# The router's logits with x as the stationary operand, in a mixture-of-experts kernel

## The reference

```python
logits = xf @ gate_w.T
scores = jax.nn.softmax(logits, axis=-1)
topv, topi = jax.lax.top_k(scores, K)        # K = 2
gates = topv / jnp.sum(topv, axis=-1, keepdims=True)
...
valid = loc < cap
flat_idx = jnp.where(valid, topi * cap + loc, 0)
...
h = jax.nn.relu(jnp.einsum('ecd,ehd->ech', de, fc1_w) + fc1_b)
eo = jnp.einsum('ech,ehd->ecd', h, fc2_w) + fc2_b
out = jnp.sum(eo.reshape(E * cap, Dm)[flat_idx] * (gates * w)[:, :, None], axis=1)
```

## Time and profile before

| | us |
|---|---|
| three runs: 1414.11, 1414.88, 1414.97; median | 1414.88 |
| the profiled execution | 1415.69 |
| its span, first to last instruction | 1413.7 |
| PE busy in the span | 1378.0 |
| last matmul of the logits ends | 42.92 |

### The profile page before, as it was taken

One profiled execution on the slowest core, in us unless ns is written; L12 is line 12 of the kernel. 1 busy time (PEld: TensorE's weight loads), 2 busy tenths in 40 slices (PEclk: granted clock), 3 DMA queues, 4 the chain that ended last, 5 costly groups with the idle time before them and its releaser, 6 DMA issues.

```text
span 1413.7 us, 18054 instructions
## 1 busy us (share of the span) xinstructions
PE 1378.0 (97%) x6175; PEld 1131.0 (80%) x6175; DVE 1053.3 (75%) x1582; ACT 705.0 (50%) x1058; POOL 314.6 (22%) x333
## 2 busy tenths in 40 slices
PE   8679999999999999999999999999999999999997
PEld 6458888888888888888888888888888888888885
DVE  6898779687877778687886878687796868865443
ACT  5456455544555445455464455454455454644442
POOL 1174203320125103221034202241032200220021
PEclk9799999999999999999999999999999999999998
DMA  8677666656457555566466565575465533543232
GB/s 286 252 175 180 131 129 178 156 115 140 106 164 172 133 99 157 150 133 146 88 187 164 106 136 133 144 162 137 90 179 148 110 75 67 156 119 69 52 104 74
DMA packets 449676, 194.41 MB, mean 138 GB/s; under 512 B 398464, under 2 KB 401673, under 8 KB 447794
## 3 DMA queue, kind: packets, MB, share of 16 engines
q1 hardware_dynamic: 427378, 125.98, 40.5%
q0 software_dynamic: 22208, 67.29, 15.3%
HBM read 153.47 MB, written 39.98 MB: 137 GB/s over the span
## 4 chain that ended last, share of the span: by engine, by line
PE 95%; DVE 3%; DMA 1%; issue 1%; ACT 0%; SPq 0%; POOL 0%; POOLq 0%
PE ps L1253 15%; PE ps L1257 15%; PE ps L1263 15%; PE ps L1228 14%; PE ps L1229 14%; PE ps L1230 14%; PE ps L1171 1%; PE ps L1244 1%; PE ps L1245 1%; PE ps L1246 1%; DVE yfull L958 1%; PE ps L1151 1%; PE ps L1152 1%; DMA x_all<-in_x 0%; DVE yfull L971 0%
## 5 line engine op out<-in xcount | busy, mean ns | idle before, releaser
L1228 PE MATMUL ps<-yc_hi,w1c_hi 128*128 128x512 f32 x896 | 349.5, 390 | 1.2 <-DVE yc_lo L924 1.2
L1230 PE MATMUL ps<-yc_hi,w1c_lo 128*128 128x512 f32 x896 | 348.7, 389 | 0.0
L1229 PE MATMUL ps<-yc_lo,w1c_hi 128*128 128x512 f32 x896 | 348.6, 389 | 0.0
L1253 PE MATMUL ps<-w_hi,h_hi 128*128 128x512 f32 x952 | 254.4, 389 | 0.0
L1257 PE MATMUL ps<-w_hi,h_lo 128*128 128x512 f32 x952 | 254.4, 389 | 0.0
L1263 PE MATMUL ps<-w_lo,h_hi 128*128 128x512 f32 x952 | 254.4, 389 | 0.0
L1263 PEld LDWEIGHTS ps<-w_lo,h_hi 128*128 128x128 f32 x952 | 178.7, 188 | 37.2
L1253 PEld LDWEIGHTS ps<-w_hi,h_hi 128*128 128x128 f32 x952 | 178.7, 188 | 37.1
L1257 PEld LDWEIGHTS ps<-w_hi,h_lo 128*128 128x128 f32 x952 | 178.7, 188 | 37.0
L1228 PEld LDWEIGHTS ps<-yc_hi,w1c_hi 128*128 128x128 f32 x896 | 168.1, 188 | 39.2 <-DVE yc_lo L924 2.2
L1230 PEld LDWEIGHTS ps<-yc_hi,w1c_lo 128*128 128x128 f32 x896 | 168.2, 188 | 35.3
(11 more groups left out here) (182 smaller groups left out, 1506.4 us busy)
## 6 DMA issues: line engine op xcount, KB each, us to landing
w_raw<-in_L_ffn_fc_w SPq DMA_DIRECT2D x232, 256.0 KB, 3.0
w_raw<-in_L_ffn_fc_w SPq DMA_DIRECT2D x512, 64.0 KB
slots_dram<-x_blk POOLq DMA_DIRECT2D x28, 512.0 KB, 3.8
x_blk<-slots_dram SPq DMA_DIRECT2D x224, 64.0 KB, 2.6
out<-x_all SPq DMA_DIRECT2D x8, 1024.0 KB, 13.0
x_all<-in_x SPq DMA_DIRECT2D x6, 1024.0 KB, 13.7
b_bc<-in_L_ffn_fc_b POOLq DMA_DIRECT2D x8, 256.0 KB, 3.8
x_all<-in_x SPq DMA_DIRECT2D x4, 256.0 KB, 3.8
```

Of the source, the lines that this page charges most:

```text
L1228: pe.matmul(bank, hi, yc_hi[:, y, q, :], start=first and q == 0, stop=False, skip_group_check=True)
L1229: pe.matmul(bank, hi, yc_lo[:, y, q, :], start=False, stop=False, skip_group_check=True)
L1230: ins = pe.matmul(bank, lo, yc_hi[:, y, q, :], start=False, stop=last and q == 1, skip_group_check=True)
L1253: pe.matmul(eo_s[:, b, :], h_hi[:, c, blk], w2_hi[:, w, :], start=False, stop=False, skip_group_check=True)
```

## The change

In the x stage the operands change places: each 128 tokens of `xT_hi` and `xT_lo` become the stationary operand and the 16 columns of `grot_hl` the moving one. A unit then has eight matmuls with 16 columns for two with 512, and the logits come out with tokens on the partitions, each in its place of the bank. `keep_logits`, `turn_logits` and their semaphores go. The last chunk's logits go to another bank (`logits_last`), so that DVE can sum the first seven chunks before it.

Beside it: the tables of the comparisons are bf16 (`wt_bf`, `first_f`, `chosen`); the scan and the counts ahead are done for each choice by itself; the last of the four parts is cut in two; SP holds the loads of w1's third pair of tiles until the gathered rows are in; `w1_low_parts(1, 0)` goes ahead of `rotate_ps(0)`; in the first two groups some banks change (`bank_c11`, `bank_p5`), the seed of group 1 and its second product come earlier, one seed of fc2's output comes later, and the fifth product of group 1 waits for `h_ready` 3.

```diff
+    PARTS = ((0, 0, JH), (0, JH, TJ), (1, 0, JH), (1, JH, TJ - JH // 2), (1, TJ - JH // 2, TJ))
...
+        def bank_c11(G):
+            return BANK_P5 if G == 1 else BANK_C11
+        def bank_p5(G):
+            return BANK_P5 if G else BANK_FIRST
...
             load_w1(1)
+            for arrived in x0_in:
+                sp.wait_ge(arrived, 16)
             load_w1(2)
             cut_x(0)
...
-                if u % Q == Q - 1 and u >= Q:
-                    keep_logits(u // Q - 1)
-            keep_logits(CHUNKS - 1)
+            act.wait_ge(xT_used, UNITS)
...
             seed_c11(0)
+            seed_c11(1)
...
+                    if G == 1:
+                        act.wait_ge(c12_done, 1)
+                        seed_eo(0, SB - 1)
...
-            dve.wait_ge(logits_T, CHUNKS)
-            link(dve.tensor_reduce(lg[:, :, :], logits_hl.rearrange("p j a e -> p j e a"), X, ALU.add))
+            for g, js, parts in ((CHUNKS - 1, slice(0, TJ - XC), logits_hl[:, 0:TJ - XC]),
+                                 (CHUNKS, slice(TJ - XC, TJ), logits_last)):
+                dve.wait_ge(xT_used, g * Q)
+                link(dve.tensor_reduce(lg[:, js, :], parts.rearrange("p j a e -> p j e a"), X, ALU.add))
+                link(dve.reduce_max(mx[:, js], lg[:, js, :], X))
...
-                link(dve.tensor_tensor(wt[:, :, :], wt[:, :, :], first_bc, ALU.mult))
+                link(dve.tensor_tensor(wt_bf, wt_bf, first_bc, ALU.mult))
...
+                dve.tensor_tensor_scan(cnt[:, k * E:(k + 1) * E, :].rearrange("p e j -> p (e j)"),
...
+            for k in range(TOPK):
+                of_k = slice(k * E, (k + 1) * E)
+                dve.wait_ge(ahead_ready, k + 1)
+                link(dve.tensor_tensor(cnt[:, of_k, :], cnt[:, of_k, :], ahead_ps[k].unsqueeze(2).to_broadcast([P, E, TJ]), ALU.add))
+                ins = dve.tensor_tensor(loc[:, of_k, :], cnt[:, of_k, :], hot[:, k, :, :], ALU.mult)
...
+            w1_low_parts(1, 0)
             rotate_ps(0)
-            w1_low_parts(1, 0)
             rotate_ps(1)
...
+            y_low(0, T3, y12)
             y_sum(0, 3)
-            y_low(0, T3, y12)
...
-                pe.matmul(bank, grot_hl[:, q, :], xT_hi[:, u % XBUF, :], start=(q == 0), stop=False)
-                pe.matmul(bank, grot_hl[:, q, :], xT_lo[:, u % XBUF, :], start=False, stop=(q == Q - 1)).then_inc(xT_used, 1)
+                for t in range(XC):
+                    at = (u // Q * XC + t) * 2 * E
+                    to = xp_all[:, at:at + 2 * E] if u < UNITS - Q else hp[:, 0, t * 2 * E:(t + 1) * 2 * E]
+                    tokens = slice(t * P, (t + 1) * P)
+                    pe.matmul(to, xT_hi[:, u % XBUF, tokens], grot_hl[:, q, :], start=(u in (0, UNITS - Q) and t == 0), stop=False,
+                              skip_group_check=True)
+                    ins = pe.matmul(to, xT_lo[:, u % XBUF, tokens], grot_hl[:, q, :], start=False, stop=(q == Q - 1), skip_group_check=True)
+                ins.then_inc(xT_used, 1)
...
             pe.wait_ge(counts_ready, 1)
-            pe.matmul(ahead_ps, before[:, :], cnt[:, :, TJ - 1], start=True, stop=False)
-            pe.matmul(ahead_ps[:, E:2 * E], ones[:, :], cnt[:, 0:E, TJ - 1], start=False, stop=True).then_inc(ahead_ready, 1)
+            pe.matmul(ahead_ps[1], ones[:, :], cnt[:, 0:E, TJ - 1], start=True, stop=False)
+            pe.matmul(ahead_ps[0], before[:, :], cnt[:, 0:E, TJ - 1], start=True, stop=True).then_inc(ahead_ready, 1)
+            pe.wait_ge(counts_ready, 2)
+            pe.matmul(ahead_ps[1], before[:, :], cnt[:, E:2 * E, TJ - 1], start=False, stop=True).then_inc(ahead_ready, 1)
...
+                if G == 1:
+                    pe.wait_ge(h_ready, 3)
+                product(S1, T1, G % 2, ps[:, bank_p5(G), :], True, False, p5_done)
...
-                    if G:
+                    if G > 1:
                         p2(G)
...
                     if G:
                         p5(G)
+                    else:
+                        p2(G + 1)
```

More of the change, by code:

```diff
@@ L127, in program @@
         first_i = sb("first_i", [P, E], I32, where=early)
-        first_f = sb("first_f", [P, E], where=early)
+        first_f = sb("first_f", [P, E], BF16, where=early)
+        chosen = sb("chosen", [P, TOPK, TJ], BF16, where=early)
         spaced = sb("spaced", [P, BLOCKS, 2], BF16, where=early)
@@ L186, in program @@
         logits_hl = xp_all.rearrange("p (j a e) -> p j a e", a=2, e=E)
-        ahead_ps = hp[:, 0, 0:TOPK * E]
+        logits_last = hp[:, 0, 0:XC * 2 * E].rearrange("p (j a e) -> p j a e", a=2, e=E)
+        ahead_ps = [hp[:, k, 0:E] for k in range(TOPK)]
         token_ps = hp[:, 0, 0:2 * BLOCKS].rearrange("p (a q) -> p a q", a=2)
@@ L534, in _ @@
             act.wait_ge(part_ready, 1)
-            for c in range(2 * TOPK):
-                k, pairs = c // 2, slice(c % 2 * JH // 2, (c % 2 + 1) * JH // 2)
+            for c, (k, begin, end) in enumerate(PARTS):
                 act.wait_ge(hot_t_ready, c + 1)
-                act.activation(hot_q[:, k, pairs, 1, :, :], hot_t[:, c % 2, :, :, :], ACT.Copy, scale=part_f[:, :]
+                act.activation(hot_q[:, k, begin // 2:end // 2, 1, :, :], hot_t[:, c % 2, 0:(end - begin) // 2, :, :], ACT.Copy,
+                               scale=part_f[:, :]
                                ).then_inc(hots_p_ready, 1)
@@ L583, in seed_c11 @@
                 act.wait_ge(p1_done, G + 1)
[L584 to L588, removed]
+                if G < 2:
                     act.wait_ge(b1_kept, 1)
                     act.wait_ge(bits_set, 1)
-                act.activation(ps[:, BANK_C11, :], running(G), ACT.Identity, bias=b1T[:, e * HT + 2 * g:e * HT + 2 * g + 1]
+                elif G == 2:
+                    act.wait_ge(h_ready, 1)
+                elif g:
+                    act.wait_ge(h_ready, e * STEPS + 2 * g - 1)
+                else:
+                    act.wait_ge(sums_ready, SB * (2 * e - 1) + BANK_C11 + 1)
+                act.activation(ps[:, bank_c11(G), :], running(G), ACT.Identity, bias=b1T[:, e * HT + 2 * g:e * HT + 2 * g + 1]
                                ).then_inc(c11_seeded, 1)
@@ L597, in keep_c11 @@
                     await_step(act, N - 3)
-                act.activation(h_hi[:, N % 3, :], ps[:, BANK_C11, :], ACT.Relu).then_inc(h_hi_ready, 1)
+                act.activation(h_hi[:, N % 3, :], ps[:, bank_c11(N // STEPS * GROUPS + N % STEPS // 2), :], ACT.Relu
+                               ).then_inc(h_hi_ready, 1)
             def seed_eo(s, b):
@@ L663, in _ @@
                     elif g < GROUPS - 1:
[L664 removed]
+                        if G:
+                            seed_c11(G + 1)
                     else:
@@ L671, in _ @@
                         act.wait_ge(bits_set, 2)
-                        for b in range(SB):
+                        for b in range(SB - 1):
                             seed_eo(0, b)
@@ L847, in _, with of_pairs @@
             link(dve.scalar_tensor_tensor(b_f[:, :, :], block_f[:, :, :], -float(P), place[:, :, :], ALU.mult, ALU.add))
[L849 to L856, removed]
+            for c, (k, begin, end) in enumerate(PARTS):
+                js, pairs, m = slice(begin, end), slice(begin // 2, end // 2), (end - begin) // 2
+                def of_pairs(ap, width):
+                    return ap.rearrange("p (m t) -> p m t", t=2).unsqueeze(2).to_broadcast([P, m, width, 2])
+                numbers = value[:, :, :].unsqueeze(1).to_broadcast([P, m, P, 2])
+                blocks = spaced[:, :, :].unsqueeze(1).to_broadcast([P, m, BLOCKS, 2])
+                table = hot_t[:, c % 2, 0:m, :, :]
                 if c >= 2:
@@ L1198, in _ @@
             idle(12)
-            for c in range(2 * TOPK):
+            for c, (k, begin, end) in enumerate(PARTS):
                 pe.wait_ge(hots_ready, c + 1)
                 pe.wait_ge(hots_p_ready, c + 1)
-                for j in range(c % 2 * JH, (c % 2 + 1) * JH):
-                    ins = pe.matmul(token_ps, hot_b[:, c // 2, j // 2, :, j % 2], hot_q[:, c // 2, j // 2, :, :, j % 2],
-                                    start=(c == 0 and j == 0), stop=(c == 2 * TOPK - 1 and j == TJ - 1))
+                for j in range(begin, end):
+                    ins = pe.matmul(token_ps, hot_b[:, k, j // 2, :, j % 2], hot_q[:, k, j // 2, :, :, j % 2],
+                                    start=(c == 0 and j == 0), stop=(c == len(PARTS) - 1 and j == TJ - 1))
                 ins.then_inc(hots_used, 1)
@@ L1323, in p2 @@
                 pe.wait_ge(c11_seeded, G + 1)
-                product(A12, B21, G % 2, ps[:, BANK_C11, :], False, True, p2_done)
+                product(A12, B21, G % 2, ps[:, bank_c11(G), :], False, True, p2_done)
             def p5(G):
@@ L1346, in _ @@
                         pe.wait_ge(yt_done, 3)
-                        set_bits(range(EO[0], EO[0] + SB))
+                        set_bits(range(EO[0], BANK_FIRST))
                         keep_warm(1)
```

(2 more changed lines are left out.)

74 lines of the change are left out of this document (25 added, 49 removed).

## The result

The changed kernel takes **1452.16 us** (median of four runs, 1448.09 to 1457.7) against 1414.93 of the kernel before beside it: 1.0263 times as long, 95% interval 1.0251 to 1.0274. The forecast was 1457, slower, range 1416 to 1464.

A forecast was written before the change was run, and what follows sets the result against it. PE, busy 97% of the span, bounds the kernel, and delay ahead of the products moves the end one for one. 1415.69 + 46.8 (x stage) - 4.5 (head) = 1458.0, less 0.81: 1457 us, range 1416 to 1464.

The forecast's parts named there:

- The price of a pair: x stage: each 128-column load with its 16-column matmul takes 0.215 us at the low clock, 0.107 at the high.
- rival B: x stage: pairs as short as 0.061 us at the high clock from 13.95 us on; kernel 1408.0 us; chance 0.17.
- The clock: x stage: low level throughout, as likelier than not; logits end at 89.8 us, +46.8 us; chance 0.57.
- Rival A: x stage: low level until 13.95 us, then high; stage +9.3 us, kernel 1419.7 us; chance 0.18.
- Rival C: x stage: the clock changes level within the stage; kernel 1424 to 1450 us, middle 1438; chance 0.08.
- What the head gives back: Router and first groups, behind the x stage's matmuls: all savings and costs together, -4.5 us.
- Logits to first comparison: Between x stage and router: only the last four tiles' sum and a maximum remain, 0.45 us for 2.30; -1.85 us.
- The bf16 tables: Router comparisons on DVE: the two products get faster in bf16, -0.27 us.
- The scan: Router on DVE: one scan of 1.23 us becomes two of about 0.70; +0.16 us.
- The counts ahead: Router, second scan to place sum: 1.85 us for 2.61, DVE using the wait for the first choice's halves; -0.75 us.
- The five parts: Router's last stretch: three more DVE fixed costs +0.26, last burst of 8 matmuls for 16 -0.95; -0.69 us.
- The first groups: Rotations and first products: moved pieces fill waits, less a new wait at product 5 of group 1; -1.1 us (-0.3 to -2.0).

The follow-up runs named there:

- swap_only: Kernel before with only the operands of the logits exchanged and the last chunk's sum apart, no other change of the head; 1453.82 us, ratio 1.0252.
- filler_1: Changed kernel plus one useless 512-column matmul ahead of the eight pairs of each x-stage unit; 1428.15 us, ratio 1.0079.
- rest_only: Changed kernel with the old x stage put back, keeping all the other changes; 1414.13 us, ratio 0.998.
- router_only: Kernel before with the router's edits alone (bf16 tables, scan and counts in two, five parts); 1413.43 us, ratio 0.9984.
- rest_warm: rest_only with five instead of three useless matmuls ahead of each of blocks 1 to 5 of gathered rows; 1415.03 us, ratio 0.9993.
- late_only: Kernel before with only the edits of the first groups and SP's wait, x stage and router as before; 1415.04 us, ratio 0.9993.
- filler_half: Changed kernel plus one useless 512-column matmul in every second x-stage unit only; 1452.12 us, ratio 1.0263.
- filler_pairs: Changed kernel plus two useless pairs (128-column load, 16-column matmul) in each x-stage unit; 1466.78 us, ratio 1.0364.

## Why the forecast was right, and where its sizes were off

**The price of a pair** was right. The forecast took 0.215 us at the low level and 0.107 at the high one from two fp32 loads; the new pairs follow each other at 0.2135 and 0.1115. PE's timeline of the changed kernel, two pairs at each level (start, busy, line):

```profile
13.54 0.26 PE L1173 MATMUL ps<-grot_hl,xT_hi 128*128 128x16 f32 x1
13.66 0.26 PE L1175 MATMUL ps<-grot_hl,xT_lo 128*128 128x16 f32 x1
...
21.37 0.36 PE L1173 MATMUL ps<-grot_hl,xT_hi 128*128 128x16 f32 x1
21.58 0.36 PE L1175 MATMUL ps<-grot_hl,xT_lo 128*128 128x16 f32 x1
```

A matmul's own record is 0.26 or 0.36 us long, and they overlap: the distance of the starts is the price. The prices are averages over the eight pairs of a unit. They exclude rival B, which needed less than 0.09 us at the high level.

**The clock** was right as the likelier case and too simple as a number. A stage at the low level from its first pair to its last exists (swap_only's profile), but both profiles of the changed kernel entered it high and fell within it. Against the forecast's 89.8 us the logits end 12.0 earlier: 9.9 of it is the entry, where the turns of unit 4 begin at 10.58 instead of 12.64 and six units run at 1.31 us or little more and a seventh partly, instead of 2.57; 2.0 are the turns, which cost 0.77 us a unit in the stream and not 0.85, so that a low unit is 2.47 (20 of them from 20.75 to 70.22 us). This is the term of the sum that was mis-sized: +34.9 for +46.8 in this execution, +44.0 in swap_only's.

**Rival A** was right about the price at the high level and wrong about getting there. filler_1 shows it: less its 32 useless matmuls of 0.23 us, 1428.15 is 1420.8, where A said 1419.7. That is an estimate, as no run holds the high level without them. By it, of the 38 us between the changed kernel and rest_only some 7 are the exchange (1420.8 less 1414.13), and some 31 the clock. The Trainium skill's page TensorE: Matmul & The Clock Gate, section Why this matters for your kernels, asks for no idle gaps between bursts of matmuls to stay at full clock. In the trace that is not enough: PE is busy, with turns, loads and 16-column matmuls, in all of the 58.8 us at 0.50. Rival C, a change of level within the stage, is what both profiles of the changed kernel show; it comes so early that their times, 1448.09 and 1452.1, lie at and just above the top of C's 1424 to 1450 and in the forecast's own range of 1443 to 1464. The forecast gave C 0.08 and its own case 0.57. In the changed kernel's profiles C has the mechanism and the forecast's case the size, and that the median came out so near 1457 owes something to how early the level happened to fall.

**What the head gives back** was -4.5 and is about -2.5 in the profiled execution (32.4 less 34.9). rest_only's -2.8 has the old copies and turns, so it stands against the sum without the first term, -2.65. By its terms, from DVE's timeline of the changed kernel:

```profile
77.92 0.23 DVE L833 TENSOR_REDUCE lg<-ps 128x32 f32<-128x64 f32 x1 [4.42 <-PE ps L1175]
78.17 0.19 DVE L834 TENSOR_REDUCE st<-lg 128x4 f32<-128x32 f32 x1
78.40 0.43 DVE L840 TENSOR_TENSOR s<-lg,st 128x256 bf16<-128x256 f32 x1
78.86 0.29 DVE L841 TENSOR_TENSOR s<-s,first_f 128x256 bf16<-128x256 bf16 x1
...
80.91 0.69 DVE L848 TENSOR_TENSOR_SCAN cnt<-carry,s 128x256 f32<-128x256 f32 x1
...
83.81 0.97 DVE L848 TENSOR_TENSOR_SCAN cnt<-carry,s 128x256 f32<-128x256 f32 x1
...
86.57 1.07 DVE L860 TENSOR_REDUCE place<-loc 128x64 f32<-128x512 f32 x1
```

- Logits to first comparison: 0.57 us (77.83 to 78.40), -1.73 for -1.85. The sum of the last four tiles and the maximum stand alone ahead of it, as said.
- The bf16 tables: only the product gained, 0.43 to 0.29 us, twice, -0.28 for -0.27.
- The scan: 0.69 and 0.97 for 1.23, so +0.43 for +0.16. The second is the longer one only where an addition on POOL has just begun, as the lines below show (83.79 us, the scan at 83.81): 0.94 to 0.98 in all six profiles of that kind, 0.69 in rest_only, router_only and rest_warm, where POOL's two additions are over before the scan. swap_only's single scan takes 1.50 beside them, 1.23 before. The exchange brings DVE's comparisons closer behind the logits (0.57 us for 2.30), but not the work of ACT that POOL waits for. That POOL's additions cost the 0.28 is argued from this; no run took them away.
- The counts ahead: the place sum starts 1.79 us behind the second scan, forecast 1.85, before 2.61; -0.82 for -0.75.
- The three together, with what overlaps: first comparison to place sum 8.17 us, before 9.01; -0.84 for -0.86.
- The five parts: the place sum to the gather is 13.91 us (86.57 to 100.48) for 14.88, -0.97 for -0.69; the prediction gives no row for the +0.26 in its sum. The last burst is PE's eight matmuls of L1219, 0.64 us, where 16 took 1.90.

POOL beside the second scan of the changed kernel (start, busy, line):

```profile
83.79 0.46 POOL L393 TENSOR_TENSOR ex_sums<-ex 128x128 f32<-128x128 f32 x1 [1.76 <-ACT ex L536]
84.32 0.55 POOL L394 TENSOR_TENSOR ex_sums<-ex_sums 128x64 f32<-128x64 f32 x1
```

**The first groups** are where this sum failed: -1.1 forecast, and in the profiled execution +0.37 from the gather to the first matmul of fc2 (100.48 to 142.27 us, 41.79, for 41.42 before, 69.11 to 110.53) and another +0.66 behind it. Two things make that up. One is the wait at product 5 of group 1, which the forecast saw coming and had within its -1.1. PE's timeline of the changed kernel, then of late_only, which names what ends the same wait, a result of DVE:

```profile
142.27 1.09 PE L1269 MATMUL ps<-w_hi,h_hi 128*128 128x512 f32 x4
...
146.84 0.47 PE L1244 MATMUL ps<-yc_hi,w1c_hi 128*128 128x512 f32 x1 [0.31 <-issue]
```

```profile
113.26 0.47 PE L1250 MATMUL ps<-yc_hi,w1c_hi 128*128 128x512 f32 x1 [0.40 <-DVE h_lo L998]
```

From the first matmuls of fc2 to the next ones it is 8.77 us (142.27 to 151.04), before 8.16 (110.53 to 118.69): 0.61 us, nearly all of the 0.66. An idle of 0.30 to 0.70 us stands at this place in all nine profiles of kernels with the edits, and in none of the three without.

The other is the clock, which the forecast did not have here: in the low stretch from 117.8 to 121.0 us the rotation's 32 matmuls take 8.85 us instead of 7.07. Two profiles with the same edits have the rotation and the products at the high level, filler_half and filler_pairs: 40.31 us (103.75 to 144.06) and 40.26 (120.05 to 160.31) from the gather to fc2. From filler_half, PE's timeline and its clock:

```profile
119.37 7.14 PE L1237 MATMUL ps<-x_turned,rows 128*128 128x256 f32 x32 [2.06 <-ACT x_turned L621]
...
144.06 1.07 PE L1271 MATMUL ps<-w_hi,h_hi 128*128 128x512 f32 x4
```

```profile
111.20:144.00 32.80, 28.48 (x132) 22.01 (x131) 31.12 (x52) 20.85 (x33) 23.30 (x24) 1.00 0.66 157
```

So with the clock up the moved pieces do bring about 1.1 us up to fc2, the wait at product 5 takes 0.6 of it back, and some -0.5 is left of the -1.1. These are single profiles; in times, late_only cannot tell -1.1 from nothing.

**Left open**: why the same stream of pairs keeps the high level for some 8 us in one execution, 5.5 in another and is low from its first pair in a third (in filler_pairs' profile it even rises there: the first loads of the stage take 0.33 us, those from 11.5 us on 0.19); and how the low stretches behind the gather can be kept away from the first groups. The best versions measured are rest_only (0.998) and router_only (0.9984), which their intervals do not separate; both leave the operands of the logits as they were.

## What to carry to other kernels

Price an exchange of operands by the columns that must be loaded against the columns that are moved: 128 loaded for 16 moved cost 0.11 us for 128 tokens, where 16 loaded for 512 moved had cost 0.23 for 512, so this exchange nearly doubled the time of PE's matmuls for the logits at the same clock (0.89 us a unit for 0.46) and saved 1.7 us behind them. Then ask at which clock the new stream runs, from a stretch of the same kind in the trace: a stage can keep PE busy without a gap and run at half speed, and the clock here cost some four times what the exchange did, by the estimate above. When such a stage can't be avoided, try one long useless matmul in each round of it, and compare times, since fewer may give nothing.

## What the runs showed of the hardware

- 32 useless matmuls of 512 columns (7.4 us of PE) took 24 us off the kernel by holding the granted clock at 1.00; 16 of them took nothing off (1452.12).
- PE and its weight loads busy in 58.80 of 58.80 us had a granted clock of 0.50; the 8.00 us ahead, as full and of the same instructions, 1.00.
- A low stretch of 3 to 7 us behind the gather stands at another place from profile to profile, of the same kernel too: 117.8 to 121.0 us and 118.5 to 125.1 in the two of the changed kernel. In it the rotation's 32 matmuls take 8.85 and 10.05 us, without it 7.1.
- The profile of swap_only records a granted clock of 1.00 over the x stage, though all its loads take 333 ns; the durations tell the level there, not the record.
- A scan of 256 values on DVE took 0.69 us, and 0.94 to 0.98 in the six profiles in which an addition on POOL had begun 0.02 to 0.05 us before it; POOL's next addition then took 0.55 us, and 0.29 where no scan ran (rest_only, router_only).
